# Loading two weight streams of a fused MLP alternately through two DMA queues

## The chip, the cores and the metric

The kernel runs on all 8 cores of one Trainium2 chip, one launch, with the same program on every core; each core works on 2 of the 16 sequences. The metric is device microseconds of the slowest core. Nothing is exchanged between cores.

## The reference, cut to what matters

Four blocks run one after the other on a stream of 16 x 2048 x 1024: attention, an MLP with ternary weights, attention again, and a tree-routed MLP with attention. The change touches the second block alone:

```
Wq = sign(W / gamma) * min(round(|W / gamma|), 1),  gamma = mean(|W|) + 1e-6
h  = x @ Wq_fc.T              # 1024 -> 4096
h  = gelu(h)
h  = layernorm(h over 4096)
y  = h @ Wq_proj.T            # 4096 -> 1024
```

## The kernel before

Each engine runs its own copy of one emitted program, in the order in which the text emits it. The helper `Prog` counts six semaphores: one for each of the compute engines (TensorE `pe`, ScalarE `act`, VectorE `dve`, GpSimd `gp`) and one for each of the two DMA queues, `dsp` for the loads that SyncE issues ("sync") and `dgp` for those that GpSimd issues ("gpsimd"). Two habits of the helper matter here. `Prog.dma` always adds a wait for the queue's own count, so each queue has one load in flight at a time. And `Prog._wait` raises every wait on a DMA semaphore to all loads emitted so far on that queue, whichever load was asked for:

```
if s in ("dsp", "dgp"):
    v = self.c[s]
```

The MLP is `emit_l0_ffn`, run once for each of the two sequences of a core. Its ternary weights lie in bf16 in two DRAM tensors, `wfcq_dram` (1024 x 4096) and `w2q_dram` (4096 x 1024). The 2048 tokens are taken in 8 groups `g` of 256. In each group the loop `for hc in range(32)` walks over the 4096 hidden columns in steps of 128. One pass of that loop emits, in this order:

- when `hc` is a multiple of 4, a load of the first weight for four passes (`hc4 = hc // 4`): 1 MB, in pieces of 1 KB, into one of the two halves of `wst` (`bpar = hc4 % 2`). It waits until the last matmul that read this half is done (`b1hg_mmB`).
- `hg_gelu(hc)`: 8 matmuls of 128x256 on TensorE that wait for the load above (`b1wfB`), at every pass, and a Gelu on ScalarE into `hgs`.
- `sq_part(hc - 1)`: the square of the pass before, on GpSimd.
- `stats(hc - 2)`: two matmuls that sum the values and the squares.
- `amm(hc - 3)`: four matmuls of 128x512 with the second weight. Its first 16 slices stay in the buffer (`w2r`). Slices 16 to 31 come in pairs, `b2_ = (hc - 16) // 2`, into one of two halves of `w2s`; `amm` waits for `b1w2B` of its half.
- when `hc` is 16 or more and even, a load of such a pair: 512 KB in pieces of 2 KB. It waits until `amm` has used the half (`b1A_mmB`).

In the kernel before, all eight loads of the first weight in a group go through SyncE, which does nothing else in the loop, and all eight pairs of the second weight go through GpSimd, where they stand in one line with the squares. After the 32 passes a tail follows: two small loads `st<-arena` on SyncE, four rank-1 matmuls, and the scaling and normalising of two token tiles on VectorE and ScalarE; then the next group begins.

Below, pass n is the loop at hc = n, "first-weight load k" is the one with hc4 = k, and "pair k" the one with b2_ = k. All matmuls are recorded at line 109, activations at 119, tensor-tensor operations at 130, and loads at 126.

Of the kernel before, what the change touches and what calls it, by code (L numbers as in the profile page):

```python
# [228 lines left out]
def a3(ap, a, b):  # L229
    return ap.rearrange("p (a b) -> p a b", a=a)  # L230
# [1622 lines left out]
def emit_l0_ffn(p, h, seq, tail_cb=None, prelude=False):  # L1853
# [12 lines left out]
    wfq = d["wfcq_dram"].rearrange("(c p) m -> p c m", p=P)  # L1866
# [34 lines left out]
    for g in range(8):  # L1901
        ts0, ts1 = g * 256, g * 256 + 256
        w2v4s = [a3(a3(w2s, 2, 2048)[:, b_, :], 2, 1024) for b_ in range(2)]

        def hg_gelu(hc):
            hc4, hci = hc // 4, hc % 4
            bpar = hc4 % 2
            spar = hc % 2
            wsv4 = a3(a3(wst, 2, 4096)[:, bpar, :], 8, 512)
            wsv = a3(wsv4.rearrange("p a b -> p (a b)"), 32, 128)  # L1910
            ph = pbank(h, spar, 1)[:, 0:256]
            for dc in range(8):
                p.mm(ph, wsv[:, dc * 4 + hci, :], xn[:, dc, ts0:ts1],
                     start=(dc == 0), stop=(dc == 7),
                     wait=(p.req(f"{t0}lnq{g // 2}", f"b1wfB{bpar}") +
                           p.bkw(spar, 1))
                     if dc == 0 else ())
            p.mark(f"b1hg_mm{spar}", "pe")
            p.act(hgs[:, hc, :], ph, AF.Gelu,
                  wait=p.req(f"b1hg_mm{spar}") + p.need(f"b1A_mm{spar}"),  # L1920
                  inc="act")
            p.bkr(spar, 1, "act")
            p.mark(f"b1hg{hc}", "act")

        def sq_part(hc):
            par = hc % 2
            p.tt("gpsimd", sqslots[par], hgs[:, hc, :], hgs[:, hc, :], ALU.mult,
                 wait=p.req(f"b1hg{hc}") + p.need(f"b1sq_used{par}"), inc="gp")
            p.mark(f"b1sq{par}", "gp")

        def stats(hc):
            par = hc % 2
            hslice = hgs[:, hc, :]
            p.mm(pbank(h, 6, 1)[0:1, 0:256], h.ones64[:, 0:1], hslice,
                 start=(hc == 0), stop=(hc == 31),
                 wait=(p.req(f"b1hg{hc}", "consts_gp") +
                       (p.bkw(6, 1) if hc == 0 else [])), inc="pe")
            p.mm(pbank(h, 7, 1)[0:1, 0:256], h.ones64[:, 0:1], sqslots[par],
                 start=(hc == 0), stop=(hc == 31),
                 wait=(p.req(f"b1sq{par}") + (p.bkw(7, 1) if hc == 0 else [])),  # L1940
                 inc="pe")
            p.mark(f"b1sq_used{par}", "pe")
            p.mark(f"b1stat{hc}", "pe")

        def amm(hc):
            spar = hc % 2
            if hc < 16:
                wsrc = w2r[:, hc, :]
                ww = p.req("b1w2r", "b1w2rS")
            else:  # L1950
                b2_ = (hc - 16) // 2
                bpar = b2_ % 2
                wsrc = w2v4s[bpar][:, hc % 2, :]
                ww = p.req(f"b1w2B{bpar}")
            for t2 in range(2):
                for dh in range(2):
                    p.mm(pbank(h, 2 + 2 * t2 + dh, 1),
                         hgs[:, hc, t2 * 128:(t2 + 1) * 128],
                         wsrc[:, dh * 512:(dh + 1) * 512],
                         start=(hc == 0), stop=False,  # L1960
                         wait=(p.req(f"b1hg{hc}") + ww +
                               (p.bkw(2 + 2 * t2 + dh, 1)
                                if hc == 0 else []))
                         if (t2 == 0 and dh == 0) or hc == 0 else ())
            p.mark(f"b1A_mm{spar}", "pe")
            if hc >= 16 and hc % 2 == 1:
                p.mark(f"b1A_mmB{((hc - 16) // 2) % 2}", "pe")

        for hc in range(32):
            if hc % 4 == 0:  # L1970
                hc4 = hc // 4
                bpar = hc4 % 2
                wsv4 = a3(a3(wst, 2, 4096)[:, bpar, :], 8, 512)
                p.dma("sync", wsv4, wfq[:, :, hc4 * 512:(hc4 + 1) * 512],
                      wait=p.need(f"b1hg_mmB{bpar}") +
                      (p.req("qfc_st0", "qfc_st1")
                       if (g == 0 and hc4 < 2) else []))
                p.mark(f"b1wfB{bpar}", "dsp")
            hg_gelu(hc)
            if hc % 4 == 3:  # L1980
                p.mark(f"b1hg_mmB{(hc // 4) % 2}", "pe")
            if hc >= 1:
                sq_part(hc - 1)
            if hc >= 2:
                stats(hc - 2)
            if hc >= 3:
                amm(hc - 3)
            if hc >= 16 and hc % 2 == 0:
                b2_ = (hc - 16) // 2
                bpar = b2_ % 2  # L1990
                p.dma("gpsimd", w2v4s[bpar],
                      w2q3[:, hc:hc + 2, :],
                      wait=p.need(f"b1A_mmB{bpar}") +
                      (b0gate if (g == 0 and b2_ < 2) else []) +
                      (p.req("qw2_st0", "qw2_st1")
                       if (g == 0 and b2_ < 2 and seq == 0) else []))
                p.mark(f"b1w2B{bpar}", "dgp")
        sq_part(31)
        stats(30)
        stats(31)  # L2000
# [64 lines left out]
def emit_all(p, h, blocks):  # L2065
    emit_load_consts(p, h)
    arn_ap = h.arn.ap
    for seq in range(NSEQ):
        emit_load_stream(p, h, seq)
        cb1 = cb2 = cb3 = None  # L2070
        if 0 in blocks:
            if 1 in blocks:
                cb1 = emit_prenorm_stats(p, h, f"b1_{seq}ln",
                                         arn_ap[:, 24832:25856])
            emit_l0_attn(p, h, seq, tail_cb=cb1)
        if 1 in blocks:
            if 2 in blocks:
                cb2 = emit_prenorm_stats(p, h, f"b2_{seq}ln",
                                         arn_ap[:, 24832:25856])
            emit_l0_ffn(p, h, seq, tail_cb=cb2, prelude=cb1 is not None)  # L2080
        if 2 in blocks:
            if 3 in blocks:
                cb3 = emit_prenorm_stats(p, h, f"b3_{seq}ln",
                                         arn_ap[:, 30976:32000])
            emit_l1_attn(p, h, seq, tail_cb=cb3, prelude=cb2 is not None)
        if 3 in blocks:
            emit_l1_ffn(p, h, seq, prelude=cb3 is not None)
        emit_store_stream(p, h, seq)
    p.do("sync", lambda e: e.wait_ge(p.sems["dsp"], p.c["dsp"]))
    p.do("gpsimd", lambda e: e.wait_ge(p.sems["dsp"], p.c["dsp"]))  # L2090
# [51 lines left out]
```

How the kernel before makes its waits and increments, by code:

```python
    def _wait(self, e, wl):  # L46
        for s, v in wl:
            if v <= 0:
                continue
            if s in ("dsp", "dgp"):
                v = self.c[s]
            if self.waited.get(s, -1) >= v:
                continue
            e.wait_ge(self.sems[s], v)
            self.waited[s] = v
# [18 lines left out]
    def do(self, engname, fn, wait=(), inc=None, n=1):  # L74
# [5 lines left out]
        elif engname == "tensor":  # L80
            if inc is None:
                inc = own
            if STRICT:
                wait = list(wait) + [(own, self.c[own])]
        if engname == self.cur:
            e = self.eng[engname]
            self._wait(e, wait)
            ins = fn(e)
            if inc is not None and ins is not None:
                ins.then_inc(self.sems[inc], n)
        if inc is not None:
            self.c[inc] += n
# [1972 lines left out]
def emit_all(p, h, blocks):  # L2065
# [13 lines left out]
                                         arn_ap[:, 24832:25856])  # L2079
            emit_l0_ffn(p, h, seq, tail_cb=cb2, prelude=cb1 is not None)
        if 2 in blocks:
            if 3 in blocks:
                cb3 = emit_prenorm_stats(p, h, f"b3_{seq}ln",
                                         arn_ap[:, 30976:32000])
            emit_l1_attn(p, h, seq, tail_cb=cb3, prelude=cb2 is not None)
        if 3 in blocks:
            emit_l1_ffn(p, h, seq, prelude=cb3 is not None)
        emit_store_stream(p, h, seq)
    p.do("sync", lambda e: e.wait_ge(p.sems["dsp"], p.c["dsp"]))
    p.do("gpsimd", lambda e: e.wait_ge(p.sems["dsp"], p.c["dsp"]))
```

## Time and profile before

| | |
|---|---|
| time, median of 3 runs | 11770.16 us (11765.1 to 11771.09) |
| the profiled execution | time 11811.22 us, span 11809.7 us on the slowest core (core 6) |
| spans of the 8 cores | 11737.5 to 11809.7 us, granted TensorE clock 0.649 to 0.656 |
| TensorE matmul busy | 7636.8 us (65% of the span) |
| ScalarE, VectorE, GpSimd busy | 3751.8 us (32%), 1984.4 us (17%), 1005.9 us (9%) |
| first-weight loads `arena<-wfcq_dram` | 128 on SyncE, 1024 KB each |
| second-weight pairs `arena<-w2q_dram` | 128 on GpSimd, 512 KB each |

A line of the profile names an engine, an operation, and out<-in by the program's names. SPq is the queue of SyncE, POOL is GpSimd, DVE is VectorE, ACT is ScalarE, PE is TensorE and PEld its weight load. The granted clock is given as a share of 2.4 GHz, so that 0.50 is 1.2 GHz. A group of the MLP takes some 140 us; there are 16 of them, 8 in the stretch from 1837 to 2951 us and 8 in the one from 7489 to 8620 us.

### The profile page before, as it was taken

What the parts mean: (1) busy time and instruction counts of PE and PEld (TensorE: products, weight loads), DVE (VectorE), ACT (ScalarE), POOL (GpSimd) and SP (SyncE); (2) the same over time, 40 slices, a digit from 0 to 9 for tenths busy, and PEclk for the clock granted to TensorE, in tenths of its full rate; (3) what the DMA queues carried; (4) which work ended last, traced back from release to release, by engine and by line L of the source; (5) the groups of instructions that cost most, each with busy time, mean ns of one, the idle gap of its engine ahead of it and who ended that gap; (6) DMA issues with size and microseconds to landing.
All of it is one profiled execution on the core that took longest, in us unless ns stands there. A gap on an engine that the chain in (4) does not pass through costs nothing.

```text
span 11809.7 us, 98257 instructions; the slowest of 8 cores (11737.5 to 11809.7 us)
## 1 busy us (share of the span) xinstructions
PE 7636.8 (65%) x30918; PEld 2865.6 (24%) x31200; DVE 1984.4 (17%) x3826; ACT 3751.8 (32%) x5097; POOL 1005.9 (9%) x1529
## 2 busy tenths in 40 slices
PE   5677315665778885474646776666667888736565
PEld 2111102332311111342432111333321111124343
DVE  3111541111100002211113111211110000231122
ACT  2455201111245554121213454311123555411122
POOL 0100001111010000101001100111102000010100
PEclk7555657778755556686776555777775555668777
DMA  2000343222100000000010000222210000000000
GB/s 43 2 3 9 109 166 108 88 88 86 22 1 2 2 2 9 15 15 15 1 59 13 2 3 10 74 95 91 93 24 4 2 2 2 9 16 15 15 1 29
DMA packets 237591, 397.05 MB, mean 34 GB/s; under 512 B 27041, under 2 KB 171425, under 8 KB 234018
## 3 DMA queue, kind: packets, MB, share of 16 engines
q0 software_dynamic: 70256, 176.32, 6.0%
q1 hardware_dynamic: 166834, 214.44, 5.8%
q8 instruction: 268, 4.39, 0.2%
q14 instruction: 233, 1.91, 0.1%
HBM read 403.41 MB, written 33.56 MB: 37 GB/s over the span
## 4 chain that ended last, share of the span: by engine, by line
PE 53%; DVE 12%; DMA 11%; ACT 11%; issue 7%; POOL 4%; DVEq 1%; ACTq 0%; POOLq 0%; SPq 0%
PE pall L109 52%; ACT pt L119 6%; DMA arena<-w2q_dram 4%; ACT arena L119 4%; POOL pt L130 3%; DVE st L157 3%; DVE arena L130 2%; DVE arena L139 1%; DVE stream L130 1%; DMA arena<-l0f_w2T 1%; DVE arena L154 1%; ACT pall L119 1%; PE pall L115 1%; DVE arena L142 1%; DVE st L130 1%
## 5 line engine op out<-in xcount | busy, mean ns | idle before, releaser
L109 PE MATMUL pall<-arena 128*128 128x256 bf16 (+7 forms) x19158 | 4637.1, 390 | 1755.5 <-ACT arena L119 541.2
L109 PEld LDWEIGHTS pall<-arena 128*128 128x128 bf16 (+2 forms) x19360 | 1808.6, 109 | 4403.4 <-issue 3854.4
L119 ACT ACTIVATE pt<-pall,cbias 128x1024 bf16<-128x1024 f32 (+7 forms) x2048 | 1926.6, 941 | 1877.5 <-PE pall L109 1854.4
L109 PE MATMUL pall<-pt,arena 128*65 128x512 bf16 (+5 forms) x6016 | 2076.9, 461 | 439.7 <-DVE pt L130 183.0
L119 ACT ACTIVATE arena<-pall 128x256 bf16<-128x256 f32 (+3 forms) x1162 | 536.4, 462 | 2801.3 <-PE pall L109 2690.2
L109 PEld LDWEIGHTS pall<-pt,arena 128*65 128x65 bf16 (+2 forms) x6016 | 560.7, 123 | 1892.1 <-issue 1833.6
L130 POOL TENSOR_TENSOR pt<-arena 128x256 bf16<-128x256 bf16 (+2 forms) x656 | 668.5, 1019 | 2824.6 <-ACT arena L119 2335.2
L109 PE MATMUL pall<-pt,ones 128*1 128x256 bf16 (+2 forms) x896 | 342.5, 437 | 420.7 <-ACT pt L119 262.4
L130 DVE TENSOR_TENSOR arena<-pall,pt 64x1024 bf16<-64x1024 f32 x128 | 155.8, 1217 | 2528.4 <-ACT pt L119 2521.7
L109 PE MATMUL pall<-arena,pt 128*128 128x512 bf16 (+2 forms) x2032 | 419.1, 346 | 149.2 <-ACT pt L119 118.7
L115 PE MATMUL pall<-ident,pt 128*128 128x128 bf16 x1284 | 157.1, 307 | 543.9 <-DVE pt L146 194.9
L119 ACT ACTIVATE pt<-pall,st 128x256 bf16<-128x256 f32 x384 | 182.1, 474 | 828.7 <-PE pall L109 828.4
L126 POOL DMA_DIRECT2D arena<-l_wo x4 | 3.7, 935 | 3919.4 <-DVE arena L130 2749.2
L115 PE MATMUL pall<-ident,arena 128*128 128x128 bf16 (+1 forms) x416 | 71.8, 285 | 396.5 <-DVE arena L154 234.3
L157 DVE TENSOR_REDUCE st<-pall 128x1 f32<-128x1024 f32 (+2 forms) x88 | 107.5, 1221 | 1298.9 <-PE pall L109 1292.1
L139 DVE TENSOR_SCALAR arena<-pall 128x64 f32<-128x64 f32 (+1 forms) x80 | 21.0, 262 | 1764.3 <-PE pall L109 1757.5
L119 ACT ACTIVATE pt<-pall 64x1024 bf16<-64x1024 f32 (+1 forms) x192 | 249.7, 1301 | 152.2 <-PE pall L109 140.2
L130 DVE TENSOR_TENSOR pt<-pt,diag 128x128 bf16<-128x128 bf16 x512 | 115.6, 226 | 1076.9 <-ACT pt L119 1073.4
L130 DVE TENSOR_TENSOR pt<-pt,pall 128x256 bf16<-128x256 bf16 x384 | 161.7, 421 | 764.2 <-PE pall L109 605.2
L119 ACT ACTIVATE arena<-pall,st 128x512 bf16<-128x512 f32 (+1 forms) x208 | 176.0, 846 | 324.0 <-PE pall L109 282.0
L109 PEld LDWEIGHTS pall<-arena,pt 128*128 128x128 bf16 (+1 forms) x2112 | 192.6, 102 | 341.3 <-issue 234.4
L115 PEld LDWEIGHTS pall<-ident,pt 128*128 128x128 bf16 x1284 | 126.8, 140 | 574.5 <-issue 574.5
(104 smaller groups left out, 3047.0 us busy)
## 6 DMA issues: line engine op xcount, KB each, us to landing
arena<-wfcq_dram SPq DMA_DIRECT2D x128, 1024.0 KB
arena<-w2q_dram POOLq DMA_DIRECT2D x128, 512.0 KB, 4.1
arena<-l0f_wfcT POOLq DMA_DIRECT2D x8, 2048.0 KB, 9.7
arena<-l0f_wfcT SPq DMA_DIRECT2D x8, 2048.0 KB
arena<-l0f_w2T SPq DMA_DIRECT2D x32, 512.0 KB
arena<-l0f_w2T POOLq DMA_DIRECT2D x32, 512.0 KB, 4.1
y_out<-stream SPq DMA_DIRECT2D x4, 4096.0 KB
stream<-x_in SPq DMA_DIRECT2D x2, 4096.0 KB
```

Of the source, the lines that this page charges most:

```text
L109: return t.matmul(out, lhsT, rhs, start=start, stop=stop)
L115: return t.transpose(out, in_, ident)
L119: self.do("scalar", lambda s: s.activation(out, in_, func, bias=bias, scale=scale, accum_out=accum_out), wait=wait, inc=inc)
L126: self.do(q, lambda e: e.dma_start(out=out, in_=in_), wait=list(wait) + chain, inc=inc, n=16)
L130: self.do(eng, lambda v: v.tensor_tensor(out, a, b, op), wait=wait, inc=inc)
L139: self.do(eng, lambda v: v.tensor_scalar(out, in0, s1, None, op0, accum_out=accum_out), wait=wait, inc=inc)
L142: self.do(eng, lambda v: v.tensor_scalar(out, in0, s1, s2, op0, op1, accum_out=accum_out), wait=wait, inc=inc)
L154: self.do(eng, lambda v: v.tensor_copy(out, in_), wait=wait, inc=inc)
L157: self.do(eng, lambda v: v.tensor_reduce(out, in_, AX.X, op, negate=negate), wait=wait, inc=inc)
```

## The change

Both streams alternate between the queues. First-weight loads with even hc4 stay on SyncE, those with odd hc4 go to GpSimd. Pairs of the second weight with even b2_ go to SyncE, those with odd b2_ stay on GpSimd. The marks name the semaphore of the queue that carries the load. The bytes, the buffers and the places where the loads are emitted stay as they are.

```
             if hc % 4 == 0:
                 hc4 = hc // 4
                 bpar = hc4 % 2
                 wsv4 = a3(a3(wst, 2, 4096)[:, bpar, :], 8, 512)
-                p.dma("sync", wsv4, wfq[:, :, hc4 * 512:(hc4 + 1) * 512],
+                p.dma("sync" if bpar == 0 else "gpsimd", wsv4,
+                      wfq[:, :, hc4 * 512:(hc4 + 1) * 512],
                       wait=p.need(f"b1hg_mmB{bpar}") +
                       (p.req("qfc_st0", "qfc_st1")
                        if (g == 0 and hc4 < 2) else []))
-                p.mark(f"b1wfB{bpar}", "dsp")
+                p.mark(f"b1wfB{bpar}", "dsp" if bpar == 0 else "dgp")
...
             if hc >= 16 and hc % 2 == 0:
                 b2_ = (hc - 16) // 2
                 bpar = b2_ % 2
-                p.dma("gpsimd", w2v4s[bpar],
+                p.dma("sync" if bpar == 0 else "gpsimd", w2v4s[bpar],
                       w2q3[:, hc:hc + 2, :],
                       wait=p.need(f"b1A_mmB{bpar}") +
...
-                p.mark(f"b1w2B{bpar}", "dgp")
+                p.mark(f"b1w2B{bpar}", "dsp" if bpar == 0 else "dgp")
```

## Rows read from the trace of the kernel before

**Rows 1.** Windows of the two MLP stretches: us, busy us by engine, PEclk, DMA share, GB/s.
```profile
1837.00:2951.00 1114.00, 665.64 (x3552) 339.70 (x3614) 142.58 (x239) 167.53 (x385) 204.84 (x320) 0.80 0.30 90
7489.00:8620.00 1131.00, 697.89 (x3682) 355.96 (x3746) 154.48 (x260) 189.38 (x406) 204.83 (x320) 0.76 0.28 89
```

**Rows 2.** TensorE's waits, 1836 to 2951 us: us, times, longest.
```profile
PE pall L109 <- DMA arena<-w2q_dram: 216.0, 55, 7.5
PE pall L109 <- ACT arena L119: 113.9, 15, 17.4
PE pall L109 <- DMA arena<-wfcq_dram: 107.5, 11, 26.9
```

**Rows 3.** The same, 7489 to 8620 us.
```profile
PE pall L109 <- DMA arena<-w2q_dram: 216.2, 57, 5.6
```

**Rows 4.** Timeline, passes 15 to 17: start us, us, engine, line, op, [idle <-releaser].
```profile
2430.50 0.27 PE L109 MATMUL pall<-arena,ones 128*1 128x256 bf16 x1
2430.70 0.36 SPq L126 DMA_DIRECT2D arena<-wfcq_dram  x1
...
2439.11 0.27 PE L109 MATMUL pall<-arena,ones 128*1 128x256 bf16 x1
2439.32 0.36 SPq L126 DMA_DIRECT2D arena<-wfcq_dram  x1
2439.34 0.38 ACT L119 ACTIVATE arena<-pall 128x256 bf16<-128x256 f32 x1 [1.77 <-PE pall L109]
2439.98 0.61 POOL L130 TENSOR_TENSOR pt<-arena 128x256 bf16<-128x256 bf16 x1 [1.54 <-PE pall L109]
2441.13 0.75 POOL L126 DMA_DIRECT2D arena<-w2q_dram  x1 [0.54 <-POOL pt L130]
2441.27 0.27 PE L109 MATMUL pall<-arena,ones 128*1 128x256 bf16 x1
2441.58 1.91 PE L109 MATMUL pall<-arena 128*128 128x512 bf16 x12
```

**Rows 5.** Timeline, passes 17 to 24.
```profile
2446.89 3.35 PE L109 MATMUL pall<-arena 128*128 128x512 bf16 x12 [3.09 <-DMA arena<-w2q_dram]
2447.35 0.75 POOL L126 DMA_DIRECT2D arena<-w2q_dram  x1 [2.44 <-DMA arena<-w2q_dram]
2452.71 0.36 SPq L126 DMA_DIRECT2D arena<-wfcq_dram  x1
2454.97 1.91 PE L109 MATMUL pall<-arena 128*128 128x512 bf16 x12
2456.67 0.74 POOL L126 DMA_DIRECT2D arena<-w2q_dram  x1 [2.68 <-PE pall L109]
2460.70 3.50 PE L109 MATMUL pall<-arena 128*128 128x512 bf16 x12 [3.51 <-DMA arena<-w2q_dram]
2466.17 0.74 POOL L126 DMA_DIRECT2D arena<-w2q_dram  x1 [7.36 <-PE pall L109]
2466.51 0.36 SPq L126 DMA_DIRECT2D arena<-wfcq_dram  x1
2473.72 3.19 PE L109 MATMUL pall<-arena 128*128 128x512 bf16 x11 [7.02 <-DMA arena<-w2q_dram]
```

**Rows 6.** Windows of 1 us: one load in flight, then two.
```profile
2415.00:2416.00 1.00, 1.00 (x6) 0.52 (x7) 0.00 (x0) 0.22 (x1) 0.51 (x1) 1.00 1.08 385
2472.00:2473.00 1.00, 0.00 (x0) 0.00 (x0) 0.00 (x0) 0.00 (x0) 0.00 (x0) 0.50 1.04 376
```

**Rows 7.** Timeline, the start of a group.
```profile
2522.87 0.37 SPq L126 DMA_DIRECT2D arena<-wfcq_dram  x1
2528.30 2.08 PE L109 MATMUL pall<-arena 128*128 128x256 bf16 x9 [7.78 <-DMA arena<-wfcq_dram]
```

**Rows 8.** DMA issues over the span: count, KB each, median us to landing.
```profile
arena<-w2q_dram POOLq DMA_DIRECT2D x128, 512.0 KB, 4.1
arena<-l_wk POOLq DMA_DIRECT2D x8, 512.0 KB, 5.5
arena<-l_wkv POOLq DMA_DIRECT2D x2, 512.0 KB, 5.9
```

**Rows 9.** The chain that ended last: the first half of `w2r`, 2 MB, then the second, on SyncE.
```profile
1809.24 11.27 DMA arena<-w2q_dram
1820.58 10.69 DMA arena<-w2q_dram
```

More of the change, by code:

```diff
@@ L1973, in emit_l0_ffn @@
                 wsv4 = a3(a3(wst, 2, 4096)[:, bpar, :], 8, 512)
-                p.dma("sync", wsv4, wfq[:, :, hc4 * 512:(hc4 + 1) * 512],
+                p.dma("sync" if bpar == 0 else "gpsimd", wsv4,
+                      wfq[:, :, hc4 * 512:(hc4 + 1) * 512],
                       wait=p.need(f"b1hg_mmB{bpar}") +
@@ L1977, in emit_l0_ffn @@
                        if (g == 0 and hc4 < 2) else []))
-                p.mark(f"b1wfB{bpar}", "dsp")
+                p.mark(f"b1wfB{bpar}", "dsp" if bpar == 0 else "dgp")
             hg_gelu(hc)
@@ L1990, in emit_l0_ffn @@
                 bpar = b2_ % 2
-                p.dma("gpsimd", w2v4s[bpar],
+                p.dma("sync" if bpar == 0 else "gpsimd", w2v4s[bpar],
                       w2q3[:, hc:hc + 2, :],
@@ L1996, in emit_l0_ffn @@
                        if (g == 0 and b2_ < 2 and seq == 0) else []))
-                p.mark(f"b1w2B{bpar}", "dgp")
+                p.mark(f"b1w2B{bpar}", "dsp" if bpar == 0 else "dgp")
         sq_part(31)
```

## The prediction

> **What bounds the kernel now.** I read the windows of the two MLP stretches first, then TensorE's waits in them, then one group in the timeline, then the load sizes. The stretches last 1114 and 1131 us [rows 1], 2245 us for 16 groups, 140 us each. TensorE sets their pace: VectorE and ScalarE work 13 and 15% of the time, and the DMA engines are busy 0.30 of it, so bytes are not short on average. What TensorE waits for is single loads. The list of waits gives 216.0 us for the second weight in the first stretch and 216.2 us in the other [rows 2, 3]. That is 27.0 us per group, in some seven waits (55 over eight groups), and it is all that the change can win, 16 x 27.0 = 432 us. The wait at the start of a group, 7.78 us for first-weight load 0 [rows 7], stands behind the two small loads of the tail. It stays, as load 0 remains on SyncE in the same place. The waits for ScalarE at the start of a group stay too.
>
> The waits for the second weight come from the rule that a wait for a load means all loads emitted on its queue. amm(18) in pass 21 needs pair 1, but pair 2 has been emitted on the same queue in pass 20, behind amm(17). So the row shows pair 2 issued at 2456.67, and TensorE resuming at 2460.70 after 3.51 us [rows 5].
>
> First-weight loads are waited for nowhere inside a group. SyncE stands ready and issues them as soon as the half is free: load 4 goes out at 2430.70, 0.20 us after the end of hg(11), which row 2430.50 marks [rows 4], and is wanted only four passes later.
>
> **The clock of a pass.** I count from T, the end of the 8 matmuls of a pass, where the first stats matmul starts. At full clock a pass lasts 2441.27 - 2439.11 = 2.15 us. amm starts at T + 0.31 and the block of 12 matmuls lasts 1.91 us, half of it the four of amm (equal columns), so amm ends and the next hg starts at T + 1.26 [rows 4]. GpSimd is later: its square of pass 15 starts at T + 0.87, and a load behind it is issued at T + 2.02 (2441.13) [rows 4]. A load held up by amm alone is issued on GpSimd 0.75 us after amm ends (2454.97 + 0.95 = 2455.92, issued 2456.67); one held up by the load before it, about 0.5 us after that landed (2446.89 to 2447.35) [rows 5]. On SyncE the same costs 0.2 us.
>
> **Prices of a load.** A pair alone takes 4.03 us from its issue to TensorE's restart [rows 5]; I use 4.0. A first-weight load alone on SyncE takes 5.4 us (2522.87 to 2528.30) [rows 7]. On GpSimd's queue no such load is shown. Nearest is `l_wkv`, in as many pieces, 5.9 us, and `l_wk` 5.5 us [rows 8]; I take 5.9, with 5.4 and 8.0 as ends. Two loads at once share one rate: 385 GB/s with one in flight, 376 with two [rows 6]. Pair 3 with load 7 beside it took 7.0 us, for 1.57 MB together (4.1 us at 385 GB/s, so 2.9 us fixed) [rows 5]. Two first-weight loads together, 2.1 MB, are then 5.5 + 2.9 = 8.4 us for the last. The one that started first gets 8.0. The ends are 5.4 (it is served first) and 10.7, the row for 2 MB in one load [rows 9].
>
> The Trainium skill ("DMA: Bandwidth & Descriptors", section "Anatomy of one DMA — SWDGE (gpsimd) path") gives such a load 2.0 us plus its bytes at 436 GB/s, an estimate of 4.4 us for 1 MB. By that the four loads on GpSimd would cost so little more that the group would lose only about 7 us. The trace speaks for more, 5.4 us on SyncE [rows 7].
>
> **Part by part, one group after the change.** What is removed: amm of an even pair waits for SyncE's queue and finds its own pair landed long ago; amm of an odd pair finds only older loads on GpSimd. All seven waits go, -27.0 us.
>
> What is added: first, four first-weight loads (1, 3, 5, 7) on GpSimd, emitted before sq_part of the same pass. GpSimd can't run ahead: it reaches load k = hc4 only after the square of two passes before.
> - Loads 1 and 3 (passes 4, 12): issued T + 2.02 after hg(hc - 2), wanted at T + 2.15 + 1.26 = 3.41. SyncE issues the next even load 0.35 us later, since its half comes free at hg(hc - 1), so both are in flight. Wait 2.02 + 8.0 - 3.41 = 6.6 us each, 13.2.
> - Load 5 (pass 20) stands behind pair 1, issued T + 2.0 after hg(17), landed + 4.0, then + 0.5: issued at 6.5, wanted at 2 x 2.15 + 1.26 = 5.56. Wait 6.5 + 5.9 - 5.56 = 6.8 us.
> - Load 7 (pass 28) stands behind pair 5, which waits for amm(23): + 0.75 + 4.0 + 0.5 = 5.25 after it, wanted after hg(27), stats and amm(24), at 2.2. Wait 5.25 + 5.9 - 2.2 = 8.95 us.
>
> Second, hg of the next pass now waits for a pair that shares its queue and was emitted after the last amm: no work lies between.
> - hg(23) (load 5, GpSimd) finds pair 3, issued 0.75 after amm(19), beside load 6 on SyncE. Pair 0 issued at 2441.13, behind load 5 at 2439.32, let TensorE restart at 2446.89, 5.76 us [rows 4, 5]; I take 5.7. Wait 6.45 us, between 4.75 and 7.75.
> - hg(25) (load 6, SyncE) finds pair 4 behind amm(21): 0.2 + 4.0 = 4.2 us; ends 3.0 and 5.6 for a pair on SyncE's queue, which no row shows.
> - hg(31) (load 7, GpSimd) finds pair 7 behind amm(27): 0.75 + 4.0 = 4.75 us.
> Passes 17, 21, 27 and 29 find nothing open on their queue.
>
> Sum: 13.2 + 6.8 + 8.95 + 6.45 + 4.2 + 4.75 = 44.35 us, less 27.0, is +17.35 us per group; 16 groups give +278 us. What hides nothing: SyncE's two pairs in front of load 6 delay it to about 4.4 us after amm(17); load 6 is wanted in pass 24, and the wait in pass 23 covers it. If that cover were gone it would cost 1 or 2 us there. The GpSimd squares behind the held loads are wanted two passes later and lose nothing.
>
> The clock: after a wait the 12 matmuls take 3.35 or 3.50 us, not 1.91 [rows 5], and the granted clock is 0.50, that is 1.2 GHz, in the window after TensorE had stood still [rows 6]. So each wait costs some 1.5 us beyond itself. There are seven before and seven after, so I put the difference at nothing; two more or fewer per group would be 3 us x 16 = 48 us.
>
> The profiled execution took 11811 us and gives 11811 + 278 = 12089. The median shown is 41 us below it, so I forecast 12048 us.
>
> **The rivals.**
> (a) Faster: the doubling of queues hides the loads. The mechanism is that the 27.0 us go and a first-weight load on GpSimd lands almost within the lead that it has. With one price x for these four loads the waits sum to 2(x - 1.4) + (x + 0.95) + (x + 3.05) + 15.4 = 4x + 16.6. That is under 27.0 only for x under 2.6 us. Half as many bytes take 4.0. If x were 2.0 the kernel would gain 38 us and take 11732. What would have to hold is that GpSimd gets to its loads passes earlier than its squares let it; its waits in the rows speak against that. The Trainium skill ("Perfetto Trace Analysis", section "DMA Optimizations") says that spreading loads over the issuing engines may help when issuing is the bottleneck; here SyncE's issue takes 0.36 us, eight of them 2.9 us in a group of 140 us [rows 4].
> (b) Slower, but less: the load issued first is served first (5.4), and pairs on SyncE take 3.0. The waits are 8.0 + 6.3 + 7.0 + 4.75 + 3.0 + 4.75 = 33.8 (load 7 shortened by 1.5 us, since TensorE at the low clock reaches it later). +6.8 per group, +109, 11879 us.
> (c) Slower still: two loads at once behave as the 2 MB load, 10.7, a load alone on GpSimd takes 8.0, pairs 7.0 and 5.4. The waits are 18.6 + 8.9 + 11.05 + 7.75 + 5.6 + 4.75 = 56.7. +29.7 per group, +475, 12245 us.
> (d) No change: the new waits happen to add up to 27. It would take all the lower ends and one wait missing.
>
> **How the numbers follow.** Forecast (between +150 and +400) 0.72, (b) 0.12, (c) 0.08, (d) 0.03, (a) 0.05. The range reaches most of the way to (b) and (c): 11890 to 12230. A measurement of this kernel tells about 0.2%, 24 us, from no change. Faster 0.05, same 0.03, slower 0.92.
>
> **What would show it.** The waits of TensorE for `w2q_dram` before an amm disappear. In their place come, per group, four waits for `wfcq_dram` of 6 to 9 us in passes 4, 12, 20 and 28, and three for `w2q_dram` of 4 to 7 us before an hg in passes 23, 25 and 31. First-weight loads on GpSimd have a landing time of 6 to 8 us. The stretches grow from 1114 and 1131 us to about 1253 and 1270, and nothing outside them moves. I am wrong if GpSimd issues its first-weight loads well before the square of two passes earlier ends, or if two loads in flight don't slow each other.

## The result, and the profile after

The changed kernel takes 12149.28 us (median of 9 runs, 12121.43 to 12202.34) against 11753.54 us (10 runs, 11712.05 to 11771.09): ratio 1.0342, 95% interval 1.0321 to 1.0362. The forecast was 12048 us in a range of 11890 to 12230, slower with a chance of 0.92. The medians are 396 us apart, where the sum had said 278. The profiled executions, from which the rows below are read, are 11811.22 and 12170.17 us, 359 us apart: the one before lies 58 us above its median, the one after 21. Some executions run in a slower state, with a lower granted clock on some of the cores; the ratios leave these out, while the medians given beside them take all runs.

The stretches of the MLP (windows; us, busy us of PE, PEld, DVE, ACT, POOL, PEclk, DMA share, GB/s), cut at the same places of the program as [rows 1]:

```profile
1842.00:3136.00 1294.00, 692.17 (x3549) 342.19 (x3611) 142.60 (x239) 167.04 (x385) 210.57 (x320) 0.73 0.24 78
7656.00:8969.00 1313.00, 709.31 (x3675) 354.32 (x3738) 154.65 (x261) 187.33 (x405) 210.54 (x320) 0.73 0.24 77
```

They last 2607 us where [rows 1] have 2245: +362, where the spans differ by 358. So the loss lies in the MLP. Outside it little moved: the stretch between the two is 18 us shorter, the one behind the second 9 us longer, the one ahead of the first 4 us longer. The work is the same and the granted clock fell from 0.80 and 0.76 to 0.73.

TensorE's waits in the first of them, to be read beside [rows 2] (us in total, times, longest):

```profile
PE pall L109 <- DMA arena<-wfcq_dram: 312.3, 39, 10.1
PE pall L109 <- DMA arena<-w2q_dram: 121.7, 24, 7.4
```

The waits for the second weight fell from 216.0 to 121.7 us, 55 times to 24, three per group. Those for the first weight rose from 107.5 to 312.3; of the 107.5, 26.9 are the one wait ahead of the first group, which the window after the change doesn't take in, so that 80.6 is the figure to compare.

One group in the timeline: its first-weight loads on GpSimd, one that SyncE issues beside them, and every restart of TensorE behind a load after the one that starts the group:

```profile
2501.86 0.92 POOL L126 DMA_DIRECT2D arena<-wfcq_dram  x1 [0.54 <-POOL pt L130]
2502.38 0.37 SPq L126 DMA_DIRECT2D arena<-wfcq_dram  x1
2510.33 1.87 PE L109 MATMUL pall<-arena 128*128 128x256 bf16 x8 [6.57 <-DMA arena<-wfcq_dram]
2512.64 3.59 PE L109 MATMUL pall<-arena 128*128 128x512 bf16 x12
2516.61 1.91 PE L109 MATMUL pall<-arena 128*128 128x512 bf16 x12
...
2529.07 0.92 POOL L126 DMA_DIRECT2D arena<-wfcq_dram  x1 [0.54 <-POOL pt L130]
2537.99 1.86 PE L109 MATMUL pall<-arena 128*128 128x256 bf16 x8 [7.42 <-DMA arena<-wfcq_dram]
2559.12 0.92 POOL L126 DMA_DIRECT2D arena<-wfcq_dram  x1 [3.12 <-DMA arena<-w2q_dram]
2565.45 1.87 PE L109 MATMUL pall<-arena 128*128 128x256 bf16 x8 [7.36 <-DMA arena<-wfcq_dram]
2580.62 1.87 PE L109 MATMUL pall<-arena 128*128 128x256 bf16 x8 [5.90 <-DMA arena<-w2q_dram]
2590.94 1.30 PE L109 MATMUL pall<-arena 128*128 128x256 bf16 x8 [3.95 <-DMA arena<-w2q_dram]
2602.19 0.92 POOL L126 DMA_DIRECT2D arena<-wfcq_dram  x1 [3.15 <-DMA arena<-w2q_dram]
2608.53 1.87 PE L109 MATMUL pall<-arena 128*128 128x256 bf16 x8 [9.39 <-DMA arena<-wfcq_dram]
2610.84 2.48 PE L109 MATMUL pall<-arena 128*128 128x512 bf16 x12
2621.82 1.87 PE L109 MATMUL pall<-arena 128*128 128x256 bf16 x8 [5.07 <-DMA arena<-w2q_dram]
```

Read them by their shape. A restart that used to begin with 12 matmuls (amm, then hg, as in [rows 5]) now begins with the 8 matmuls of an hg. All seven of these waits sit there, in passes 4, 12, 20, 23, 25, 28 and 31, in the order that the prediction gave. A POOL load whose idle time ends at "POOL pt L130" stood behind a square; one that ends at "DMA arena<-w2q_dram" stood behind a pair. Over the whole span a first-weight load on GpSimd lands 6.7 us after its issue in the median, where 6 to 8 were expected.

### The profile page after: what moved, and what is told of

It reads as the page before. It is cut to its first block, busy times and chain, and to the rows that moved or that the text cites. A ratio compares the mean times of both kernels' runs of the same rounds, so it can differ in the third digit from the quotient of the medians.

```text
span 12167.5 us, 98184 instructions; the slowest of 8 cores (12106.9 to 12167.5 us)
## 1 busy us (share of the span) xinstructions
PE 7660.8 (63%) x30918; PEld 2860.6 (24%) x31200; DVE 1984.9 (16%) x3826; ACT 3750.1 (31%) x5097; POOL 1020.1 (8%) x1529
## 3 DMA queue, kind: packets, MB, share of 16 engines
q14 instruction: 233, 1.91, 0.1%
## 4 chain that ended last, share of the span: by engine, by line
PE 52%; DMA 14%; DVE 12%; ACT 11%; issue 7%; POOL 4%; DVEq 1%; ACTq 0%; POOLq 0%; SPq 0%
PE pall L109 51%; ACT pt L119 6%; DMA arena<-wfcq_dram 4%; ACT arena L119 4%; POOL pt L130 3%; DMA arena<-w2q_dram 3%; DVE st L157 2%; DVE arena L130 2%; DVE arena L139 1%; DVE stream L130 1%; DMA arena<-l0f_w2T 1%; DVE arena L154 1%; ACT pall L119 1%; PE pall L115 1%; DVE arena L142 1%
## 5 line engine op out<-in xcount | busy, mean ns | idle before, releaser
L130 POOL TENSOR_TENSOR pt<-arena 128x256 bf16<-128x256 bf16 (+2 forms) x656 | 668.6, 1019 | 3615.0 <-ACT arena L119 2997.0
L130 DVE TENSOR_TENSOR arena<-pall,pt 64x1024 bf16<-64x1024 f32 x128 | 155.8, 1217 | 2528.0 <-ACT pt L119 2521.4
L157 DVE TENSOR_REDUCE st<-pall 128x1 f32<-128x1024 f32 (+2 forms) x88 | 107.5, 1221 | 1303.0 <-PE pall L109 1296.2
L130 DVE TENSOR_TENSOR pt<-pt,diag 128x128 bf16<-128x128 bf16 x512 | 115.6, 226 | 1077.1 <-ACT pt L119 1073.7
L130 DVE TENSOR_TENSOR pt<-pt,pall 128x256 bf16<-128x256 bf16 x384 | 161.9, 422 | 748.7 <-PE pall L109 590.9
```

The lines of the kernel that those rows point to most:

```text
L130: self.do(eng, lambda v: v.tensor_tensor(out, a, b, op), wait=wait, inc=inc)
L157: self.do(eng, lambda v: v.tensor_reduce(out, in_, AX.X, op, negate=negate), wait=wait, inc=inc)
```

## The experiments

Two edits recur. "Exact waits" means that inside the group loop a wait for a load uses the count of that load, not of every load emitted on its queue:

```
-            if s in ("dsp", "dgp"):
+            if s in ("dsp", "dgp") and not self.exact:
                 v = self.c[s]
...
+    p.exact = True
     for g in range(8):
```

Ratios are to the kernel before, in the same batch on the same chip. Group lengths are means over whole groups of the first stretch (six, but five for e2 and e3 and four for e1), from one small tail load `st<-arena` to another.

**Part one alone: first-weight loads.** Only the first hunk of the change. Label e1.

> The kernel before, with only the first-weight loads alternating (odd ones on GpSimd); all pairs of the second weight stay on GpSimd. Theory (a load on GpSimd stands behind the squares of earlier passes, and a wait takes in every load emitted on its queue): waits of 6 to 9 us in passes 4, 12, 20 and 28, the waits before amm stay, and hg in passes 21, 23, 29 and 31 waits some 4.8 us more for a pair. Waits sum to about 54 us per group against 27 to 29 before, and with the low clock behind the extra waits a group grows by some 34 us: about 12300 us, ratio 1.045. Rival (it is the spread of the pairs, or the mere use of two queues by both streams, that costs): less than the whole change, ratio 1.00 to 1.02.

Measured 12356.67 us, ratio 1.0497 (1.044 to 1.0553). Restarts behind loads in one group, from the timeline, after the one that starts it:

```profile
2383.77 1.86 PE L109 MATMUL pall<-arena 128*128 128x256 bf16 x8 [7.32 <-DMA arena<-wfcq_dram]
...
2439.29 1.86 PE L109 MATMUL pall<-arena 128*128 128x256 bf16 x8 [5.88 <-DMA arena<-wfcq_dram]
2448.00 1.87 PE L109 MATMUL pall<-arena 128*128 128x256 bf16 x8 [4.80 <-DMA arena<-w2q_dram]
...
2487.15 1.87 PE L109 MATMUL pall<-arena 128*128 128x256 bf16 x8 [4.83 <-DMA arena<-wfcq_dram]
```

Twelve waits, 55.2 us together, where 54 was expected: four for first-weight loads, four before amm and four of 4.7 to 4.8 us for pairs before hg. Loads 5 and 7 waited less than the 6 to 9 us expected, 5.88 and 4.83. This half alone loses more than the whole change.

**Part two alone: the pairs.** Only the second hunk. Label e2.

> The kernel before, with only the pairs of the second weight alternating; all first-weight loads stay on SyncE. Theory: the waits before amm vanish; hg in passes 21, 25 and 29 waits about 4.2 us each for a pair emitted on SyncE, 12 to 13 us per group against 27 to 29. A group shrinks by 15 us and by some 5 us of low clock: about 11440 us, ratio 0.973. Rival (two loads in flight slow each other so that nothing is won): ratio 0.995 to 1.01, with waits of 6 us and more.

Measured 11523.79 us, ratio 0.9749 (0.9665 to 0.9834). Its group in the timeline has three long waits, each before an hg, as expected:

```profile
2500.93 1.87 PE L109 MATMUL pall<-arena 128*128 128x256 bf16 x8 [3.96 <-DMA arena<-w2q_dram]
2515.99 1.87 PE L109 MATMUL pall<-arena 128*128 128x256 bf16 x8 [4.85 <-DMA arena<-w2q_dram]
2531.17 1.69 PE L109 MATMUL pall<-arena 128*128 128x256 bf16 x8 [3.99 <-DMA arena<-w2q_dram]
```

Faster than before is shown, and the rival's 0.995 is excluded; whether it is as much as 2% the interval leaves open. So the change is a gain of some 300 us (2.5%) and a loss of some 590 (5.0%) put together. Alone they sum to +2.5%, together they give +3.4%; by the times this is within the intervals. The profiles say more plainly that the two are not independent: a group lasts 140.8 us before, 175.1 in e1 (+34.2) and 122.2 in e2 (-18.6), in sum +15.6, and 162.7 with the whole change, +21.9.

**Exact waits on the changed kernel.** Label e3.

> The changed kernel, but inside the group loop a wait for a load waits for that load alone, not for every load emitted on its queue (each queue still has one load in flight, so the count is exact). Theory: the three waits of hg in passes 23, 25 and 31 (14.9 us per group) vanish, the four for odd first-weight loads (30.8 us) stay: some 19 us per group less with the clock, about 11840 us, ratio to before 1.008. Rival (the odd first-weight loads alone are the whole loss, and the pairs' waits are displaced rather than removed): little change from 12149, ratio 1.03.

Measured 11886.56 us, ratio 1.0098 (1.006 to 1.0136). The waits of hg for pairs are gone, those for odd first-weight loads stay (31.8 us in one group), and one is new, in pass 24, here between those of passes 20 and 28:

```profile
2489.56 1.87 PE L110 MATMUL pall<-arena 128*128 128x256 bf16 x8 [8.68 <-DMA arena<-wfcq_dram]
2503.84 1.87 PE L110 MATMUL pall<-arena 128*128 128x256 bf16 x8 [3.86 <-DMA arena<-wfcq_dram]
2523.31 1.86 PE L110 MATMUL pall<-arena 128*128 128x256 bf16 x8 [9.36 <-DMA arena<-wfcq_dram]
```

**Exact waits on the kernel before.** No load moved. Labels e4 and e11 (the same kernel, a second time, as the base of two runs below).

> The kernel before, no load moved, with the same exact waits. Theory: a pair is issued 0.75 us behind amm and wanted three passes later, 5.5 us on, and takes 4.0 to 7.0: of the 27 to 29 us per group some 2 stay, and the low clock behind the waits goes too (about 10 us per group). About 11200 us, ratio 0.953. Rival (the engine queue or the DMA rate sets the pace, not the rule of the waits): ratio above 0.98.

> The kernel before with exact waits, once more, as the common base of the two runs beside it on the same chip: ratio 0.953 to 0.957.

Measured 11223.47 us, ratio 0.9535 (0.9457 to 0.9613), and 11348.79 us, 0.9599 (0.9561 to 0.9637). The second lies just above what was expected for it, and its interval reaches into that range. This is the rule of the waits priced by itself: 4 to 5% of the kernel. In six groups (e4) the waits for the second weight add up to 29.5 us, 4.9 per group where 2 were expected, and 28.4 stood before:

```profile
PE pall L110 <- DMA arena<-wfcq_dram: 48.5, 6, 9.2
PE pall L110 <- DMA arena<-w2q_dram: 29.5, 24, 3.7
```

**Exact waits, and GpSimd's loads emitted earlier.** The changed kernel again, with the same queues; the odd load is emitted beside the even one before it. Label e5.

```
-            if hc % 4 == 0:
-                hc4 = hc // 4
+            if hc % 4 == 0:
+                for hc4 in ((hc // 4, hc // 4 + 1)
+                            if (hc // 4) % 2 == 0 else ()):
```

> The changed kernel with exact waits, and GpSimd's odd first-weight loads emitted four passes earlier, together with the even one before it, when their half has just come free. Same queues, same bytes. Theory (the loads came late only because GpSimd reaches them behind the squares): the four waits of some 31 us per group vanish, ratio to before about 0.955, 11220 us, the same as the kernel before with exact waits. Rival (a first-weight load costs more on GpSimd's queue, or two loads in flight cost, wherever it is emitted): ratio 0.98 to 1.01.

Measured 11379.12 us, ratio 0.9602 (0.9548 to 0.9656), against 1.0098 for e3. Moving the same loads four passes up, on the same queue, is worth 5% of the kernel. The interval holds the forecast of 0.955 and excludes the rival's 0.98. In one group, of the waits for first-weight loads only two are left, for load 0 and for load 6, both from SyncE:

```profile
2381.21 3.57 PE L110 MATMUL pall<-arena 128*128 128x256 bf16 x16 [10.14 <-DMA arena<-wfcq_dram]
2453.28 1.86 PE L110 MATMUL pall<-arena 128*128 128x256 bf16 x8 [3.98 <-DMA arena<-wfcq_dram]
```

A group lasts 110.2 us, against 107.5 in e4: the loads on GpSimd are no longer waited for, but the second queue wins nothing either.

**The squares off GpSimd.** The changed kernel, its waits and order as they are, with `sq_part` on VectorE. Label e7.

```
-            p.tt("gpsimd", sqslots[par], hgs[:, hc, :], hgs[:, hc, :], ALU.mult,
+            p.tt("vector", sqslots[par], hgs[:, hc, :], hgs[:, hc, :], ALU.mult,
```

> The changed kernel with its waits and order of loads as they are, but the squares computed on VectorE, so that GpSimd has nothing but loads in the loop and can run ahead. Theory: the waits in passes 4, 12 and 20 (some 21 us per group) vanish with the low clock behind them; load 7 still stands behind pair 5 (9.4 us), and the waits of hg in passes 23, 25 and 31 stay (15 us). About 24 us of waits per group, 28 us less than the changed kernel per group: 11700 us, ratio to before 0.995. Rival (the price of the load on GpSimd's queue, not its late issue): little change, ratio 1.02 or more.

Measured 11754.5 us, ratio 0.9938 (0.9916 to 0.9961). One group, all its restarts behind loads:

```profile
2486.99 3.43 PE L109 MATMUL pall<-arena 128*128 128x256 bf16 x16 [7.85 <-DMA arena<-wfcq_dram]
2539.95 1.03 PE L109 MATMUL pall<-arena 128*128 128x256 bf16 x8 [0.31 <-DMA arena<-w2q_dram]
2560.34 1.86 PE L109 MATMUL pall<-arena 128*128 128x256 bf16 x8 [7.32 <-DMA arena<-w2q_dram]
2570.85 1.03 PE L109 MATMUL pall<-arena 128*128 128x256 bf16 x8 [3.76 <-DMA arena<-w2q_dram]
2589.08 1.87 PE L109 MATMUL pall<-arena 128*128 128x256 bf16 x8 [9.98 <-DMA arena<-wfcq_dram]
2602.25 1.87 PE L109 MATMUL pall<-arena 128*128 128x256 bf16 x8 [4.97 <-DMA arena<-w2q_dram]
```

No wait in passes 4, 12 and 20; load 7 behind pair 5 (9.98 us) and the three waits for pairs are left. The sum of these waits behind the first is 26.3 us, where 24 was expected. e5 and e7 take the lateness away in two ways that share nothing, and both times TensorE no longer waits for the odd loads on GpSimd, but for load 7 in e7, which still stands behind pair 5. It is where they stand in GpSimd's line that costs.

**Exact waits with the pairs alternating.** Label e6.

> The kernel before with exact waits and only the pairs alternating. Theory: nearly nothing is left to win behind the exact waits, ratio 0.950 to 0.955 (11200 us). Rival (the second queue is of worth in itself): ratio 0.94 or less.

Measured 11393.7 us, ratio 0.963 (0.9597 to 0.9663): neither theory nor rival, the forecast is missed by 1%. The timeline shows why:

```profile
2447.95 1.86 PE L110 MATMUL pall<-arena 128*128 128x256 bf16 x8 [6.46 <-DMA arena<-wfcq_dram]
2461.76 1.87 PE L110 MATMUL pall<-arena 128*128 128x256 bf16 x8 [3.59 <-DMA arena<-wfcq_dram]
```

Loads 6 and 7, in passes 24 and 28, are late on SyncE, where pairs 2 and 4 stand in front of them and wait for amm. The same rows of e2, with the old waits, have no such wait in passes 24 and 28: hg stood still for a pair in passes 21 and 25.

**The same with load 6 emitted ahead of pair 2.** Label e10.

```
+            if hc == 20:
+                ld_first(6)
             if hc >= 16 and hc % 2 == 0:
```

> Exact waits with the pairs alternating, and first-weight load 6 emitted ahead of pair 2 on SyncE. Theory (what the alternation of the pairs loses behind exact waits is that pair 2, which waits for amm(17), stands in front of load 6, whose half has long been free): the wait of 6.5 us in pass 24 vanishes, that of 3.6 us in pass 28 stays, amm(20) waits 1 us; ratio 0.955 to 0.958 to before, some 110 us under the 0.963 of the version with pair 2 in front. Rival (two loads in flight slow each other): stays at 0.963.

Measured 11312.2 us, ratio 0.9588 (0.956 to 0.9615). In one group:

```profile
2438.79 1.90 PE L110 MATMUL pall<-arena 128*128 128x512 bf16 x12 [2.13 <-DMA arena<-w2q_dram]
2454.79 1.87 PE L110 MATMUL pall<-arena 128*128 128x256 bf16 x8 [6.36 <-DMA arena<-wfcq_dram]
```

The wait in pass 24 is gone. Of the 6.5 us, though, part came back: load 7 now waits 6.36 us, not 3.59, and amm 2.13. Over six groups the group fell from 111.8 to 109.2 us. The interval touches that of e6, so that by the times alone the gain isn't shown; by the place of the waits and the length of a group it is. Beside e11 on the same chip (0.9599) the alternation of the pairs wins nothing behind exact waits.

**Load 0 ahead of the tail.** Exact waits, load 0 of the next group emitted before the tail's small loads. Label e8.

> The kernel before with exact waits, and first-weight load 0 of the next group emitted ahead of the tail and its two small loads. Theory (what ends the gap between groups is the tail on VectorE and ScalarE): the wait of some 8 us for load 0 vanishes and the wait for ScalarE grows by as much; 11223 us, no change against exact waits alone (ratio 0.953). Rival (the load sets the start of a group): 8 x 14 = 110 us less, ratio 0.944.

Measured 11332.07 us, ratio 0.9579 (0.9534 to 0.9623), between e4 and e11, and above the rival's 0.944. TensorE's waits in six groups:

```profile
PE pall L110 <- ACT arena L120: 147.9, 6, 26.0
PE pall L110 <- DMA arena<-w2q_dram: 42.0, 30, 4.3
```

The six waits for load 0 (48.5 us in e4, above) are gone, and those for ScalarE are 147.9 us where e4 has 99.7: +48.2. The tail on VectorE and ScalarE ends the gap between groups, not the load. The waits for pairs rose too, by 12.5 us in the six groups; why was not looked into.

**One late load alone.** Exact waits, load 3 alone on GpSimd: a single long wait, to price what lies behind it. Label e9.

```
-                p.dma("sync", wsv4, wfq[:, :, hc4 * 512:(hc4 + 1) * 512],
+                p.dma("gpsimd" if hc4 == 3 else "sync", wsv4,
```

> The kernel before with exact waits, and first-weight load 3 alone on GpSimd, where it comes late: one wait of some 7 us per group in a stretch that has none. It prices the clock behind a single long wait. Theory (TensorE stands still so long that the clock has fallen to 1.2 GHz before the load lands, and the next 20 matmuls run at it): a group grows by the wait and 2.5 us more, 9.7 us, 155 us in all above exact waits alone. Rival (the low clock behind a wait costs nothing, as the forecast assumed between seven waits and seven): 7.2 us per group, 115 us.

Measured 11482.95 us, ratio 0.9702 (0.966 to 0.9745), 0.0103 above e11. That is some 120 us, next to the rival's 115, but each ratio is known to 0.004 only, some 50 us, so the times leave the theory's 155 open. The profiles tell them apart. Six groups, windows and waits, e9 first, then e11:

```profile
2045.61:2747.32 701.71, 470.61 (x2712) 244.21 (x2712) 110.59 (x190) 127.81 (x294) 159.33 (x246) 0.83 0.34 108
PE pall L110 <- DMA arena<-wfcq_dram: 95.2, 12, 9.6
PE pall L110 <- DMA arena<-w2q_dram: 23.5, 24, 3.7
```

```profile
2028.09:2673.40 645.31, 455.99 (x2714) 240.25 (x2712) 110.62 (x190) 127.80 (x294) 154.11 (x240) 0.85 0.38 118
PE pall L110 <- DMA arena<-wfcq_dram: 47.2, 6, 8.3
PE pall L110 <- DMA arena<-w2q_dram: 27.5, 23, 4.2
```

A group grew by (701.71 - 645.31) / 6 = 9.4 us. Waits for loads grew by (118.7 - 74.7) / 6 = 7.3 us. The other 2.1 are no wait for a load: TensorE's own busy time rose by 14.6 / 6 = 2.4 us for the same matmuls, at a mean clock of 0.83 against 0.85. So the rival, that the clock costs nothing, is refuted by the profiles, which are of one execution each.

## Why the prediction was right, and by how much it was off

**The new waits, term by term.** Forecast and the group shown above: passes 4 and 12, 6.6 each, measured 6.57 and 7.42; pass 20, 6.8, measured 7.36; pass 23, 6.45, measured 5.90; pass 25, 4.2, measured 3.95; pass 28, 8.95, measured 9.39; pass 31, 4.75, measured 5.07. The sum was forecast at 44.35 and is 45.66 us. The first hit owes something to luck. Load 1 took 8.47 us, not 8.0, but TensorE also came to it later, 3.92 us after T and not 3.41, since hg(3) still ran at the low clock behind the wait for ScalarE. e1, e2, e3 and e7 took these away in groups, and each time those vanished that the reading of the code named.

**The price of a first-weight load on GpSimd** was taken as 5.9 us alone and 8.0 beside another. The group shows 2559.12 to 2565.45, 6.3 us, alone, and 8.5 and 8.9 with SyncE's load in flight. Both are a little dearer than taken, for the most part because the two prices rest on times to landing, while all the others run from the issue to TensorE's restart. The row for pair 3 with load 7 beside it has 7.02 us as TensorE's wait, and the load's own time to landing is 7.0; from its issue at 2466.17 to the restart at 2473.72 it is 7.55 [rows 5]. With 7.55 the same working gives 3.45 us fixed and 8.95 for two first-weight loads, close to what was measured. In the same way `l_wkv`'s 5.9 is a time to landing, and the load alone landed after 6.1. The Trainium skill's fit ("DMA: Bandwidth & Descriptors", section "Anatomy of one DMA — SWDGE (gpsimd) path", 2.0 us plus bytes at 436 GB/s, an estimate of 4.4 us) lies too low for this load, by these 6.1.

**The waits that go.** Forecast: all seven, 27.0 us per group. Measured: no restart of amm is left in the group. Waits for loads in six whole groups rose from 227.5 us (170.4 for the second weight, 57.1 for the first) to 328.6 us: 16.9 per group, where 17.35 was forecast. This is the mechanism, and it held. Both sides of the difference were larger than forecast, 28.4 per group for the waits that went and not 27.0, and new ones of 45.66 in the group shown and not 44.35; in the difference the two errors all but cancel.

**The term that was mis-sized is the clock.** "Seven before and seven after, so I put the difference at nothing." The same six groups, windows before and after:

```profile
1951.38:2796.40 845.02, 505.05 (x2664) 256.28 (x2712) 110.63 (x190) 127.80 (x294) 153.61 (x240) 0.79 0.30 90
1979.00:2955.37 976.37, 522.69 (x2664) 257.99 (x2712) 110.65 (x190) 127.59 (x294) 157.89 (x240) 0.73 0.24 78
```

A group grew by 21.9 us. Waits for loads are 16.9 of it. The other 5.0, some 80 us over 16 groups, is the size of the gap between 278 and 359. Of these, 2.9 are TensorE's busy time for the same 2664 matmuls, at a granted clock of 0.73 against 0.79: this is the clock, 47 us in all. The other 2.1 are waits that the forecast had not in its sum: in six groups those for VectorE rose from 10.3 to 15.6 us, those for ScalarE from 97.5 to 101.4, and the ones that the profile calls "issue" from 3.7 to 8.0. That they come from the low clock too is likely, since several stand right behind slow matmuls, but no run shows it.

So the waits are seven and seven, and yet they don't cost the same. Two windows of 1 us after the change:

```profile
2506.00:2507.00 1.00, 0.00 (x0) 0.00 (x0) 0.00 (x0) 0.00 (x0) 0.00 (x0) 0.61 1.09 386
2515.00:2516.00 1.00, 1.00 (x6) 0.57 (x4) 0.00 (x0) 0.00 (x0) 0.00 (x0) 0.50 0.00 0
```

Before, around the restart at 2460.70 of [rows 5]:

```profile
2460.00:2461.00 1.00, 0.30 (x1) 0.13 (x2) 0.00 (x0) 0.00 (x0) 0.00 (x0) 0.90 0.01 4
2461.00:2462.00 1.00, 1.00 (x4) 0.44 (x3) 0.00 (x0) 0.00 (x0) 0.00 (x0) 0.50 0.00 0
```

Both clocks fall to 0.50, that is 1.2 GHz. Before, that happens as TensorE restarts after 3.51 us, and 12 matmuls run slowly (3.50 us). After, TensorE stands still for 6.57 us and the clock falls in the middle of that. Yet it doesn't rise until 2516, 6 us after the restart: 8 matmuls (1.87 us) and 12 more (3.59 us) run slowly, where 12 did. e9 shows the cost of one such wait without the others: 2.1 to 2.4 us. Length alone doesn't order the costs, though. The longest wait after, 9.39 us, is followed by 8 matmuls in 1.87 us and 12 in 2.48, less than behind the 6.57. Before, the 12 matmuls behind the wait of 3.61 us in pass 29 ran at the full clock:

```profile
2503.59 1.90 PE L109 MATMUL pall<-arena 128*128 128x512 bf16 x12 [3.61 <-DMA arena<-w2q_dram]
```

An estimate from the timelines of the two groups, against 1.91 us for 12 matmuls and 1.03 for the 8 of an hg at the full clock, gives 1.5 us per wait before, as the prediction put it, and 2.0 after. So the price was right for the old waits and too small for the new ones. What sets the cost of a given wait stays open; no run changed the clock alone.

**The cover.** I wrote that load 6 behind SyncE's pairs is covered by the wait in pass 23 and "would cost 1 or 2 us there" without it. e3 and e6 took the cover away, and it cost 3.86 and 6.46 us. The mechanism was right, the price was not worked out: load 6 issued 4.4 us after amm(17), taking 5.4, and wanted three passes of 2.15 later, gives 3.35 us by the prediction's own figures. In e3 load 6 went out at 2498.17 and took 5.7 us to the restart. In e6 it went out at 2440.40, with a pair on GpSimd issued at 2439.93 beside it, and took 7.5.

**The rivals.** (a), two queues hide the loads, is refuted for the emission as it stands. Its condition (GpSimd reaches the loads passes earlier) is what e5 and e7 make true. With the old waits that gives 0.9938 (e7), a gain of 0.6%; with exact waits 0.9602 (e5), no better than exact waits without any load moved. The Trainium skill's advice to spread loads ("Perfetto Trace Analysis", section "DMA Optimizations") binds itself to descriptor generation as the bottleneck; no run here had that, with issue records of 0.36 us on SyncE and 0.92 on GpSimd. (b) fails at its condition: the load that was issued first took 8.5 and 8.9 us beside another, not 5.4. (c) came nearer in the time, +475 us against the measured +396, but not by its prices: it has 10.7 where 8.5 to 8.9 were measured, 8.0 where 6.3, and 56.7 us of waits where the group has 45.66. (d), no change, would need waits of 27 us in place of these 45.66.

## What to carry to other kernels

A load on an engine that also computes is issued when that engine's line reaches it, not when its buffer is free. Before you move a load, write down which instruction stands before it and when that one can finish.

If a wait takes in everything emitted on a queue, mixing two streams on one queue ties each to the other's last load. Counting exactly, which is safe here because each queue has one load in flight, was worth more (4 to 5%) than any distribution over the queues (2.5% for the pairs alone, e2). Behind it no distribution gained anything: 0.963 and 0.9588 with the pairs alternating, 0.9602 with all loads alternating and the odd ones emitted early, 1.0098 with them emitted late, against 0.9535 and 0.9599 with no load moved.

Price a stall together with the slow matmuls behind it: here some 2 us beyond a single wait of 7 us. Read that cost from rows of the like, and not from the number of stalls.

## What the runs showed of the hardware that was not expected

The same 1 MB first-weight load moves in different packets on the two queues. Queue lines of two windows with one such load in flight, on SyncE (kernel before) and on GpSimd (after); queue, kind: packets, MB, share of 16 engines (of windows of 9 and 10 us, so the shares are not to be compared):

```profile
q1 hardware_dynamic: 1040, 1.05, 39.1%
```

```profile
q0 software_dynamic: 275, 1.05, 31.1%
```

Yet the load is no faster on GpSimd, 6.3 us to TensorE's restart against 5.4 on SyncE [rows 7]. The issue record of such a load is 0.92 us on GpSimd against 0.75 for a pair and 0.36 on SyncE.
